# An expert loop's down product from high and low parts, with routing's order changed

## The reference

```python
x = x + attention(conditional_experts(x, cond))      # 4 experts + shared, 16 heads
x = x + ffn(sequence_block(x, cond))

# sequence_block: projections B_t, C_t, u of 64 states each, gated scan, then
y = ys @ Wo + bo                                     # 64 states -> 256 channels

# ffn(x), E = 8 experts, H = 256, FFN = 1024
route = sigmoid(x @ Wr + br)
max_prob, max_ind = max(route), argmax(route)
for e in range(8):
    mask = max_ind == e
    out += mask * (gelu(x @ W1[e]) @ W2[e])
out = out * max_prob
```

## Time and profile before

| | |
|---|---|
| median of 3 runs | 753.32 us (753.28 to 753.43) |
| profiled execution | 754.85 us |
| its span | 752.9 us |
| granted TensorE clock, mean | 0.994 |
| PE busy | 733.3 us, 97% |
| DVE, ACT, GpSimd busy | 354.0, 436.4, 188.4 us |

### The profile page before, as it was taken

The page is one execution under the profiler, slowest core; times in us unless marked ns, Lnnn a source line. Parts: engine busy times, 40 slices in busy tenths (PEclk is TensorE's granted clock), DMA queues, the critical chain, the costliest instruction groups (busy, mean ns, idle before and its releaser), DMA issues.

```text
span 752.9 us, 12379 instructions
## 1 busy us (share of the span) xinstructions
PE 733.3 (97%) x4237; PEld 461.4 (61%) x4237; DVE 354.0 (47%) x743; ACT 436.4 (58%) x719; POOL 188.4 (25%) x283
## 2 busy tenths in 40 slices
PE   7999999999999999999999999999999989999996
PEld 5778888788777788743333332332338455688885
DVE  4888767728976676228433220211215751122221
ACT  4432222345423322689999999999985735344442
POOL 6344545403443341150000000000000012334442
PEclk9999999999999999999999999999999998999999
DMA  8232111100023370603363450941017723712100
GB/s 252 49 58 57 56 44 40 57 28 29 29 105 108 114 149 0 85 1 57 85 140 131 66 78 8 243 72 24 1 36 257 268 63 117 254 47 68 46 21 5
DMA packets 51965, 62.99 MB, mean 84 GB/s; under 512 B 15410, under 2 KB 43482, under 8 KB 51912
## 3 DMA queue, kind: packets, MB, share of 16 engines
q1 hardware_dynamic: 44576, 55.96, 29.1%
q0 software_dynamic: 2576, 5.25, 2.3%
q10 hardware_dynamic: 4760, 1.08, 0.7%
HBM read 50.01 MB, written 14.55 MB: 86 GB/s over the span
## 4 chain that ended last, share of the span: by engine, by line
PE 66%; ACT 19%; issue 7%; DVE 6%; DMA 1%; ACTq 0%; POOLq 0%; SPq 0%; DVEq 0%
PE psum L1586 33%; ACT pexp L803 15%; PE psum L1975 11%; PE psum L1691 6%; PE psum L1678 4%; PE psum L1962 3%; PE psum L1779 2%; PE psum L1900 2%; DVE hl L1026 2%; DVE hh L1174 1%; DMA x_tm<-in_x 1%; DVE ssum L1214 1%; PE psum L1895 1%; PE psum L1954 1%; DVE qk_tm L1246 1%
## 5 line engine op out<-in xcount | busy, mean ns | idle before, releaser
L803 ACT ACTIVATE pexp<-psum 128x1024 f32<-128x1024 f32 x256 | 236.5, 1133 | 2.7 <-PE psum L1678 2.6
L790 ACT ACTIVATE hid<-psum,b_col 128x512 f32<-128x512 f32 x96 | 66.2, 690 | 162.5 <-PE psum L1586 122.3
L1691 PE MATMUL psum<-pexp,v_ones 128*32 128x512 f32 x1024 | 136.2, 604 | 0.4 <-ACT pexp L803 0.4
L1678 PEld LDWEIGHTS psum<-q_stack,k_stack 48*128 48x128 f32 x512 | 44.0, 183 | 114.8 <-ACT pexp L803 103.5
L1026 DVE SCALAR_TENSOR_TENSOR hl<-hid,scale_col,hh 128x341 fp32r<-128x341 f32 x192 | 104.8, 587 | 3.4
L1678 PE MATMUL psum<-q_stack,k_stack 48*128 48x512 f32 x512 | 106.1, 472 | 0.0
L1174 DVE TENSOR_SCALAR hh<-hid,scale_col 128x341 fp32r<-128x341 f32 x192 | 71.8, 415 | 57.3 <-ACT hid L790 40.2
L1975 PE MATMUL psum<-w_all,fh 128*128 (+1 forms) x368 | 83.3, 380 | 0.1
L1586 PE MATMUL psum<-hh,w2h 128*128 128x512 f32 x192 | 76.6, 399 | 1.8 <-DVE hl L1026 1.7
L1586 PE MATMUL psum<-x_hi,w1h 128*128 128x512 f32 x192 | 77.0, 401 | 0.6 <-DVE x_lo L1040 0.6
L997 ACT ACTIVATE fh<-psum,b_col 128x128 f32<-128x128 f32 x184 | 50.0, 386 | 47.4 <-PE psum L1962 46.2
(11 more groups left out here) (259 smaller groups left out, 928.2 us busy)
## 6 DMA issues: line engine op xcount, KB each, us to landing
raw<-in_L_cond_ew SPq DMA_DIRECT2D x32, 256.0 KB, 3.2
parts_d<-parts SPq DMA_DIRECT2D x8, 1024.0 KB, 4.0
w_raw<-in_L_ffn_W SPq DMA_DIRECT2D x8, 1024.0 KB, 8.5
w_all<-in_L_ffn_W SPq DMA_DIRECT2D x8, 1024.0 KB, 10.9
q_stack<-parts_d SPq DMA_DIRECT2D x48, 128.0 KB, 4.6
k_stack<-parts_d SPq DMA_DIRECT2D x48, 128.0 KB, 7.0
raw<-in_L_cond_sw SPq DMA_DIRECT2D x16, 256.0 KB, 3.3
x_tm<-in_x SPq DMA_DIRECT2D x4, 512.0 KB, 8.4
```

Source lines behind the costliest of these rows:

```text
L790: act.activation(hid[k % 4][:], bank(k % 4), ACT.Gelu_apprx_tanh, bias=b1_col[:, bass.ds(4 * q + k // 2, 1)]).then_inc(gelu_done, 1)
L803: act.activation(pexp[mt % 2][:, 2 * j:2 * j + 2, 512 * h:512 * h + 512], psum[:, 2 * r:2 * r + 2, :], ACT.Exp, scale=D ** -0.5)\
L1678: ins = pe.matmul(psum[:, 2 * r + lane, :], k_stack[i][rows, j, mt * P:(mt + 1) * P], q_stack[i][rows, j, 512 * h:512 * h + 512], start=Tr ...
L1691: ins = pe.matmul(psum[VW * j:VW * j + VW, 6 + h, :], v_ones[i][:, mt, j, :], pexp[mt % 2][:, j, 512 * h:512 * h + 512], start=(mt == 0), ...
```

## The change

The down product is made with `three`, from high and low parts of W2 and of gelu's output. DVE splits gelu's output (`split_hidden`, one cast and one subtraction for each half of 512 columns). W2's parts of 2048 columns per expert are made on three engines: GpSimd makes both for experts 2 and 3 ahead of the sequence block's end; ACT makes the high part of the others (`w2_hi_part`); the low part is DVE's for experts 0, 4 and 6 and GpSimd's, in four pieces of 512, for 1, 5 and 7. The low part is written over W2 itself.

To this end the loads of W2 are issued in another order, the raw copies' places differ, one fold more lies in the loop (`FIRST_FOLDS` 7), the turned biases of experts 4 to 7 come one iteration later, and `rank` goes ahead of the first turned bias. The products for the probabilities move behind the first two up products, and their copy on DVE behind the first two copies of weights and states. SP's wait in front of W2's experts 4 to 7 is still for nine folds, the ninth of which is now made in iteration 1 of the loop instead of 0.

```diff
@@ -62,11 +62,15 @@
 ROW = C + 2 * N
-FOLDS = [("fold", 0), ("bias", 0), ("fold", 1), ("fold", 2), ("bias", 2), ("fold", 3), ("fold", 4), ("fold", 5),
-         ("bias", 4), ("fold", 6), ("bias", 6), ("fold", 7)]
+FOLDS = [("fold", 0), ("bias", 0), ("fold", 1), ("fold", 2), ("bias", 2), ("fold", 3), ("fold", 4),
+         ("fold", 5), ("bias", 4), ("fold", 6), ("bias", 6), ("fold", 7)]
 BIAS_AT = [1, 4, 8, 10]
-FIRST_FOLDS = 8
+FIRST_FOLDS = 7
 XS = 4
+EARLY_W2 = [2, 3]
+HIGH_BY_ACT = [0, 1, 4, 5, 6, 7]
+LOW_BY_DVE = [0, 4, 6]
+LOW_BY_POOL = [2, 3, 1, 5, 7]
 EARLY = 8
...
@@ -215,11 +222,13 @@
         w2_all = sb("w2_all", [P, RE, FC * C], F32, [top])
+        w2_lo = sb("w2_lo", [P, RE, FC * C], F32R, [top])
+        w2_hi = sb("w2_hi", [P, RE, FC * C], F32R, [top + RE * UNIT])
         w1_raw = [sb(f"w1_raw{e}", [P, CK, FF], F32, [top + W1_UNIT[e] * UNIT]) for e in range(RE)]
-        lane_hot = sb("lane_hot", [P, TT, P], F32R, [top + 12 * UNIT])
-        tile_hot = sb("tile_hot", [P, TT, 3, TW], F32R, [top + 13 * UNIT])
+        lane_hot = sb("lane_hot", [P, TT, P], F32R, [top])
+        tile_hot = sb("tile_hot", [P, TT, 3, TW], F32R, [top + UNIT])
         y_rows = sb("y_rows", [P, NB, LT, 2, N], F32, [top + 10 * UNIT])
...
@@ -586,8 +601,11 @@
             sp.wait_ge(av_done, LT * 2 * GROUPS)
-            for e in range(3, 6):
-                load_w1(e)
+            load_w1(3)
+            load_w2(2)
+            load_w1(4)
+            load_w2(3)
+            load_w1(5)
             load_w2(0)
@@ -595,13 +613,13 @@
             load_w2(1)
-            load_w2(2)
             sp.wait_ge(rows_stored, 16 * 2 * NB)
                 sp.wait_ge(xs_in[i], 16)
-            load_w2(3)
-            sp.wait_ge(folded, FIRST_FOLDS + 1)
+            sp.wait_ge(folded, FOLDS.index(("bias", 4)) + 1)
             for e in range(4, RE):
+                if e == 6:
+                    sp.wait_ge(probs_known, 1)
                 load_w2(e)
@@ -699,6 +717,21 @@
+            def w2_lo_part(e):
+                if e not in EARLY_W2:
+                    pool.wait_ge(w2_high, HIGH_BY_ACT.index(e) + 1)
+                for q in range(4):
+                    c = slice(512 * q, 512 * q + 512)
+                    ins = pool.tensor_tensor(w2_lo[:, RE - 1 - e, c], w2_all[:, RE - 1 - e, c],
+                                             w2_hi[:, RE - 1 - e, c].bitcast(F32), ALU.subtract)
+                ins.then_inc(w2_by_pool, 1)
+            pool.wait_ge(ctx_done, 2 * H // HG)
+            for n, e in enumerate(EARLY_W2):
+                pool.wait_ge(w2_in[e], 16)
+                pool.tensor_copy(w2_hi[:, RE - 1 - e, :], w2_all[:, RE - 1 - e, :]).then_inc(w2_early, 1)
+                pool.wait_ge(w2_early, n + 1)
+                w2_lo_part(e)
             pool.wait_ge(seq_made, 6)
@@ -715,6 +748,8 @@
+            w2_lo_part(1)
             for s in range(TILES):
@@ -723,6 +758,8 @@
                                         bounds_check=T - 1, oob_is_err=False).then_inc(out_stored[s % 2], 16)
+                if s in (3, 5):
+                    w2_lo_part(s + 2)
@@ -978,21 +1015,28 @@
             store_rows(1)
+            def w2_hi_part(e):
+                act.wait_ge(w2_in[e], 16)
+                after(act, folded, (2, 6, 0, 0, 0, 0, 11, 12)[e])
+                act.copy(w2_hi[:, RE - 1 - e, :], w2_all[:, RE - 1 - e, :]).then_inc(w2_high, 1)
             copy_fold(2)
+            copy_fold(3)
             copy_bias(0)
-            for k in range(3, 6):
-                copy_fold(k)
+            copy_fold(4)
+            w2_hi_part(0)
+            act.activation(act_warm[:], ones[0:1, 0:1], ACT.Gelu)
+            copy_fold(5)
             copy_bias(1)
             copy_fold(6)
-            act.activation(act_warm[:], ones[0:1, 0:1], ACT.Gelu)
-            copy_fold(7)
+            w2_hi_part(1)
             act.wait_ge(slots_done, 1)
                 act.wait_ge(up_done, s + 1)
-                after(act, down_done, s - 1)
+                after(act, fh_split, 2 * s - 2)
                 for f in range(FC):
@@ -1004,10 +1048,12 @@
                     gelu_tile(s + 1, place_of_expert(act, s + 1))
+                if 4 <= s + 2 < RE:
+                    w2_hi_part(s + 2)
                 if FIRST_FOLDS + s < len(FOLDS):
                     copy_fold(FIRST_FOLDS + s)
-                if s in (1, 3):
-                    copy_bias(2 + s // 2)
+                if s in (2, 4):
+                    copy_bias(1 + s // 2)
@@ -1456,10 +1502,12 @@
             dve.tensor_scalar(tile_i[:], tf[:], -1.0, float(RE - 1), ALU.mult, ALU.add).then_inc(slots_done, 1)
-            dve.wait_ge(probs_made, 1)
-            link(dve.tensor_copy(prob_s[:], bank(5)[:, TW:TW + TILES]))
-            dve.tensor_tensor(prob_s[:], bank(5)[:, 0:TILES], prob_s[:], ALU.add).then_inc(probs_known, 1)
+            def w2_lo_part(e):
+                dve.wait_ge(w2_high, HIGH_BY_ACT.index(e) + 1)
+                dve.tensor_tensor(w2_lo[:, RE - 1 - e, :], w2_all[:, RE - 1 - e, :],
+                                  w2_hi[:, RE - 1 - e, :].bitcast(F32), ALU.subtract).then_inc(w2_by_dve, 1)
@@ -1473,6 +1521,16 @@
+            def split_hidden(s, h):
+                i, f = s % 2, slice(4 * h, 4 * h + 4)
+                raw = fh[i][:, 512 * h:512 * h + 512].rearrange("p (f n) -> p f n", n=P)
+                dve.wait_ge(fh_out, 2 * s + h + 1)
+                after(dve, down_done, s - 1)
+                dve.tensor_copy(fh_hi[i][:, f, :], raw).then_inc(fh_high, 1)
+                dve.wait_ge(fh_high, 2 * s + h + 1)
+                dve.tensor_tensor(fh_lo[i][:, f, :], raw, fh_hi[i][:, f, :].bitcast(F32), ALU.subtract)\
+                    .then_inc(fh_split, 1)
@@ -1483,11 +1541,24 @@
                 copy_states(s)
+            dve.wait_ge(probs_made, 1)
+            link(dve.tensor_copy(prob_s[:], bank(5)[:, TW:TW + TILES]))
+            dve.tensor_tensor(prob_s[:], bank(5)[:, 0:TILES], prob_s[:], ALU.add).then_inc(probs_known, 1)
+            w2_lo_part(0)
+            for h in range(2):
+                split_hidden(0, h)
             for s in range(TILES):
                     copy_states(s + 2)
+                if s + 1 < TILES:
+                    for h in range(2):
+                        split_hidden(s + 1, h)
+                if s in (3, 5):
+                    w2_lo_part(s + 1)
                 dve.wait_ge(xs_in[s % XS], 16 * (s // XS + 1))
+                if s == 0:
+                    dve.wait_ge(probs_known, 1)
                 o_tile(s)
@@ -1885,8 +1956,10 @@
                     pe.wait_ge(fold_out, k - 1)
-                if k in (4, 7, 10):
-                    pe.wait_ge(bias_out, k // 3)
+                if k in (4, 10):
+                    pe.wait_ge(bias_out, 1 if k == 4 else 3)
+                elif k == FIRST_FOLDS:
+                    pe.wait_ge(probs_known, 1)
                 for f in range(e, e + 2 if what == "bias" else e + 1):
@@ -1917,7 +1990,6 @@
             fold(2)
-            turn_bias(0)
@@ -1928,9 +2000,9 @@
             rank()
-            for k in range(3, 6):
-                fold(k)
-            turn_bias(1)
+            fold(3)
+            turn_bias(0)
+            fold(4)
             pe.wait_ge(token_hot, 1)
@@ -1938,23 +2010,31 @@
             ins.then_inc(tokens_made, 1)
-            pe.wait_ge(probs_hot, 1)
-            for i in range(TT):
-                ins = pe.matmul(bank(5)[:, 0:2 * TW], lane_hot[:, i, :],
-                                tile_hot[:, i, 1:3].rearrange("p a s -> p (a s)"), start=(i == 0), stop=(i == TT - 1))
-            ins.then_inc(probs_made, 1)
-            for k in range(6, FIRST_FOLDS):
-                fold(k)
+            def probabilities():
+                pe.wait_ge(probs_hot, 1)
+                for i in range(TT):
+                    ins = pe.matmul(bank(5)[:, 0:2 * TW], lane_hot[:, i, :],
+                                    tile_hot[:, i, 1:3].rearrange("p a s -> p (a s)"),
+                                    start=(i == 0), stop=(i == TT - 1))
+                ins.then_inc(probs_made, 1)
+            fold(5)
+            turn_bias(1)
+            fold(6)
                 after(pe, fo_out, s - 2)
+                if s == 1:
+                    pe.wait_ge(fold_out, FOLDS.index(("fold", 3)) + 1)
                 pe.transpose(turned_row(s), xs[s % XS][:, C:], ident[:]).then_inc(xs_turned, 1)
                 pe.wait_ge(t_copied, s + 1)
+                if s == 0:
+                    pe.wait_ge(bias_out, 2)
                 pe.wait_ge(yT_copied, s + 1)
@@ -1967,12 +2047,15 @@
                 if s < RE:
-                    pe.wait_ge(w2_in[s], 16)
+                    if s in LOW_BY_DVE:
+                        pe.wait_ge(w2_by_dve, LOW_BY_DVE.index(s) + 1)
+                    else:
+                        pe.wait_ge(w2_by_pool, LOW_BY_POOL.index(s) + 1)
                 for f in range(FC):
                     if f % 4 == 0:
```

(20 more changed lines are left out.)

## The result

| | before | after |
|---|---|---|
| median | 753.32 us | 759.97 us (758.74 to 762.14, 7 runs) |
| ratio to before | | 1.0084, 95% interval 1.007 to 1.0099 |
| profiled execution, span | 752.9 us | 758.9 us |
| granted clock, mean | 0.994 | 0.987 |

A forecast was written before the change was run, and what follows sets the result against it. PE's array was taken as the bound. Terms of -14.3, -0.4, +1.9, +1.3, +4.1, +2.7, +4.9, +0.3 and +4.2 gave +4.7 on the profiled 754.85, so 759.5, less 1.5 for the median: 758.0 us, range 748.0 to 771.0.

The forecast's parts named there:

- The down product, -14.3: Expert loop on PE: 24 products in 2.84 us instead of 3.46, 0.62 saved per tile over 23 tiles.
- The row of the QKV product: Profile row of the V part, same helper and shape: 0.118 us per product, taken for the new down product.
- The start, -0.4: Ahead of the loop: the first down product starts at 629.5 instead of 629.96, PE idle for 4.5 us before it.
- routing's gain: Ahead of the loop: rank before the turned bias makes the work up to the moved probabilities 5 to 6 us earlier.
- The clock, +4.2: Low granted clock behind PE's long gaps: 2.6 us for the first, 0.8 each for two others; bounds 0 and 8.1.
- the three gaps: PE idle 4.5 us before the first down product, 4.1 before tile 6's transpose, 4.9 before tile 7's down product.
- Waits at tiles 5 to 8, +11.7: PE waits for W2's parts of experts 4 to 7: +4.1, +2.7 (0.5 and 2.2) and +4.9 us.
- Steady state, +1.3: Later loop tiles: period 4.27 us against PE's own 4.19, about 15 tiles at 0.08 each.
- The ring: Loop, over two tiles: up product, gelu's half, splits, output tile, then a later transpose; 8.54 us, so 4.27 per tile.
- Faster: Rival at experts 4 to 7: GpSimd and the loads keep up, no long gaps, clock stays; 747.2 us, chance 0.20.
- The second: Rival in the loop: gathers and scatters hold DVE, 12 to 24 us more; chance 0.18, shared with slow products.
- The third: Rival of near no change: PE's gaps don't lower the clock, 753.8 us, chance 0.20.

The follow-up runs named there:

- folds_in_gap: The changed kernel with folds 7 and 8 made in PE's idle time before the first down product, not in loop iterations 0 and 1: 761.03 us, ratio 1.0098.
- fill_gap: The changed kernel with eleven never-read products of 512 columns on PE behind the probabilities, before the first down product: 760.59 us, ratio 1.0085.
- o_between: The changed kernel with DVE's output tile s between the two half splits of tile s + 1, except at s = 3 and 5: 760.12 us, ratio 1.0061.
- no_w2_parts: The changed kernel without W2's parts for experts 0, 1, 4 to 7, the place read right before each down product: 753.79 us, ratio 0.9993.
- dve_57: The changed kernel with the low parts of experts 5 and 7 made by DVE in one subtraction each, not by GpSimd: 756.15 us, ratio 1.0018.

## Why the prediction held, and where it didn't

- *The down product, -14.3.* Right: 2.86 against 2.84, so -13.8. The row of the QKV product was the right one to read, and the address from a register costs nothing, as long as the register is read early; read right before the product it costs 0.5 to 0.7 per tile. The figure that the prediction took from the Trainium skill ("TensorE: Matmul & The Clock Gate", section "Back-to-back issue gap"), an estimate of 0.109 for one product of 256 columns, isn't met: 24 products would take 2.6.
- *The start, -0.4.* The mechanism was right (all of routing's gain is used up ahead of the first down product), the size was off by 2.05. The step that failed took every fold at 1.87 once the order is changed; the clock fell behind the token products, and two folds and a turned bias took 1.6 more. And the hold by GpSimd was put in the wrong place: the low part of expert 0 was to wait 0.6 for GpSimd, and instead got in ahead of GpSimd's last piece, and the cast behind it was held for 1.0.
- *The clock, +4.2.* Right in the sum, 5.0, but not in its parts: 2.6, 0.8 and 0.8 were forecast for the three gaps, and 2.5, nothing and 2.5 came. The gaps were rightly named as the cause: with the first one filled the product behind it runs at full clock. That the forecast added it to a schedule at full clock, where the kernel before had lost 2.7 to it already, is the other side of the start's error.
- *Waits at tiles 5 to 8, +11.7.* Each was there, and they were 8.1: 2.0, 1.3, 1.2 and 3.5 where 4.1, 0.5, 2.2 and 4.9 were forecast. At the transpose of tile 6 PE was free 4.8 later than forecast (658.8, not 654.0) and the output tile was done 2.7 later (660.7, not 658.0), so the wait was half as long. Ahead of down product 5 the 0.8 more is the length of GpSimd's four pieces, 4.94 instead of 4.16. W2 of expert 4 landed 5.9 after its issue and not 7.2, and DVE's low part of 2.28 was as sized. For expert 7 the forecast had GpSimd's pieces alternate with DVE's instructions until 681.0, 6.1 us; they went through in 4.92, while DVE's copy was held; no subtraction of DVE came up in that time.
- *Steady state, +1.3.* The ring was found, and sized at 4.27 for 4.41. It leaves out what a restart costs: behind a wait the down product takes 3.06, and casts beside gather or scatter took up to 0.62 instead of 0.43.
- *The rivals.* Faster came out in no run of the changed kernel. The second, gathers and scatters that hold DVE by their length, is wrong in that form: they add 0.2 at most to a cast. The port does cost, but through GpSimd's rows of subtractions. By the rule in the Trainium skill ("SBUF — State Buffer", section "Who interferes with whom") the loser is blocked for one whole instruction. In this kernel a copy or cast was held for a whole row of four (5.62), as long as nothing came between them, and with a pause for one (1.98); the measurement decides. The third, the clock stays, was wrong.

That the total came so near is partly luck, because errors of both signs met: start, steady state and clock some 4.6 more than forecast, the down product's saving 0.5 less, the waits 3.6 less.

## What to carry to other kernels

A shorter product on the bound engine is worth its difference only where each operand's maker keeps its pace; count for each tile what the makers' queues hold, not their busy shares. An engine that is nearly idle is no free place for work if it shares a port with the one that feeds the bound engine. And where PE idles for some us, look for the low clock behind it: filling one gap gives back nothing as long as the next gap takes it.

## What the runs showed of the hardware

- A copy or cast of 512 fp32 columns on DVE, 0.42 alone, is held until a row of four GpSimd subtractions ends (5.62 and 5.49 in `folds_in_gap`, 4.73 in `fill_gap`, 4.58 in `o_between`, 3.88 in the changed kernel). With a wait between the pieces the cast takes 1.9 to 2.0, and a DVE subtraction of two SBUF inputs 1.64 for 0.69.
- A DVE subtraction of 2048 columns with two SBUF inputs, begun beside the third piece of such a row, got in ahead of the fourth: it took 2.50 for 2.28, the piece 3.31 for 1.26 (changed kernel).
- A read of a register from SBUF right before the product that uses it costs 0.24 to 0.40 of idle time and 0.27 in the product (`no_w2_parts`); ahead of the transpose it costs nothing.
- A gather of 128 rows takes 7.1 to 7.8 instead of 3.1 beside four loads of 1 MB issued together (7.78 in the changed kernel, 7.08 in `folds_in_gap`).
- A gap of the same length is followed by the low clock in one run and not in another (1.58: 4.62 or 3.12 for the down product behind it; 2.8: 5.27 or 3.05).
- The mean clock of one kernel differs between executions, and the time with it: `dve_57` from 753.51 at 0.994 to 758.47 at 0.984.
